# Last Mamba item: key strips issued in three parts, the query side six states sooner, four maxima of attention in the tail

## The reference, cut to what matters

```python
x = x + mamba(layernorm(x))             # 2 layers, 512 channels, 16 states
x = x + cross_attention(layernorm(x), ctx)   # 16 heads of 16
x = x + moe(layernorm(x))               # 8 experts, top 2, and a shared one
# Mamba, per step t, channel e, state n:
v = 0.6 * v + delta * B[n] * xb
h = exp(-delta * exp(a_log)) * h + v
y = sum_n h * C[n]                      # then (y + dp * xb) * silu(z), out projection
# attention: softmax((q k^T) / 4) v, then the output projection
```

## Time and profile before

| | us |
|---|---|
| three timed runs | 1520.03, 1529.7, 1526.61 (median 1526.61) |
| profiled execution | 1523.77 |
| its span in the trace | 1522.3 |
| PE busy | 1374.1 (90%) |
| DVE busy | 1054.2 (69%) |
| ACT busy | 892.6 (59%) |
| POOL busy | 926.5 (61%) |

### The profile page before, as it was taken

One profiled execution on the slowest core, in us unless ns is written; L12 is line 12 of the kernel. 1 busy time (PEld: TensorE's weight loads), 2 busy tenths in 40 slices (PEclk: granted clock), 3 DMA queues, 4 the chain that ended last, 5 costly groups with the idle time before them and its releaser, 6 DMA issues.

```text
span 1522.3 us, 46973 instructions
## 1 busy us (share of the span) xinstructions
PE 1374.1 (90%) x20570; PEld 969.4 (64%) x20570; DVE 1054.2 (69%) x1345; ACT 892.6 (59%) x1303; POOL 926.5 (61%) x809
## 2 busy tenths in 40 slices
PE   5799999999999999999999977789898887999997
PEld 2367776776776776776776765344434344599996
DVE  4698887887887987986986895776676761522224
ACT  3767776776775786776676662145555565434440
POOL 1289989989989989989988968500303000045541
PEclk8799999999999999999999998889999999999999
DMA  5021222212221221122212354540606002512225
GB/s 171 17 75 72 82 86 86 85 59 86 113 82 62 85 86 65 78 86 86 85 59 78 135 136 131 99 95 1 121 5 110 2 1 64 222 53 68 72 63 183
DMA packets 41498, 127.28 MB, mean 84 GB/s; under 512 B 8784, under 2 KB 21584, under 8 KB 32848
## 3 DMA queue, kind: packets, MB, share of 16 engines
q1 hardware_dynamic: 34736, 108.28, 21.8%
q0 software_dynamic: 6048, 14.95, 3.7%
q10 hardware_dynamic: 512, 1.05, 0.4%
HBM read 97.90 MB, written 9.57 MB: 71 GB/s over the span
## 4 chain that ended last, share of the span: by engine, by line
PE 46%; DVE 28%; ACT 11%; issue 9%; DMA 3%; POOL 2%; SPq 2%; DVEq 0%; ACTq 0%
DVE hst L790 13%; PE psum L633 6%; PE psum L1315 4%; PE psum L1727 4%; DVE w_early L790 4%; PE psum L1739 4%; PE psum L610 3%; DVE overlay L681 3%; ACT dA L935 3%; PE psum L572 3%; PE psum L1297 2%; PE psum L507 2%; PE psum L1669 2%; PE psum L1281 2%; DMA overlay<-x_hat,origin 2%
## 5 line engine op out<-in xcount | busy, mean ns | idle before, releaser
L1004 POOL TENSOR_TENSOR hst<-hst,cb 128x512 f32<-128x512 f32 x399 | 510.5, 1304 | 94.6 <-DVE hst L790 79.9
L790 DVE TENSOR_TENSOR_SCAN hst<-dA,psum 128x512 f32<-128x512 f32 x399 | 463.5, 1202 | 108.8 <-PE psum L633 108.7
L610 PE MATMUL psum<-ident,hst 128*128 128x128 f32 x1596 | 236.2, 282 | 15.4 <-POOL hst L1004 12.7
L935 ACT ACTIVATE dA<-delta,alog 128x512 f32<-128x512 f32 x256 | 177.7, 718 | 86.2 <-DVE hst L790 65.4
L935 ACT ACTIVATE dA<-xres,alog 128x512 f32<-128x512 f32 x256 | 176.9, 718 | 70.8 <-DVE hst L790 53.6
L610 PEld LDWEIGHTS psum<-ident,hst 128*128 128x128 f32 x1596 | 174.8, 142 | 63.4 <-POOL hst L1004 21.4
L1436 DVE TENSOR_REDUCE nmax<-psum 128x2 f32<-128x1024 f32 x128 | 154.6, 1221 | 56.9 <-PE psum L1281 56.6
L1365 ACT ACTIVATE pT<-psum 128x1024 f32<-128x1024 f32 x128 | 128.0, 1024 | 103.1 <-PE psum L1301 79.7
L633 PE MATMUL psum<-filt,c_early 64*64 64x86 f32 (+1 forms) x6144 | 145.2, 239 | 20.3 <-DVE hst L790 12.2
L633 PE MATMUL psum<-filt,uT 64*64 64x86 f32 (+1 forms) x6144 | 145.1, 239 | 20.1 <-DVE hst L790 10.8
L633 PEld LDWEIGHTS psum<-filt,c_early 64*64 64x64 f32 x6144 | 124.7, 134 | 57.4 <-issue 40.5
(11 more groups left out here) (234 smaller groups left out, 2102.5 us busy)
## 6 DMA issues: line engine op xcount, KB each, us to landing
cb<-c_rows SPq DMA_DIRECT2D x64, 1024.0 KB, 4.7
qk_first<-w_early SPq DMA_DIRECT2D x64, 64.0 KB, 2.4
qk<-part SPq DMA_DIRECT2D x64, 64.0 KB, 2.7
w_up<-up_dram SPq DMA_DIRECT2D x8, 512.0 KB, 8.0
w_down<-down_dram SPq DMA_DIRECT2D x8, 512.0 KB, 13.7
w_up<-y_choice SPq DMA_DIRECT2D x8, 512.0 KB, 7.0
qk<-part POOLq DMA_DIRECT2D x48, 64.0 KB, 5.1
qk_first<-part SPq DMA_DIRECT2D x40, 64.0 KB, 2.4
```

Of the source, the lines that this page charges most:

```text
L610: m = pe.matmul(psum[:, Y0 + et % EP, t * P:(t + 1) * P], hst(i)[:, t * P:(t + 1) * P], ident[:], start=n == 0 and t == 0, stop=n == NSTAT ...
L790: dve.tensor_tensor_scan(hst(i), a, v, 0.0, ALU.mult, ALU.add).then_inc(scan_done, 1)
L935: act.activation(dA[:, a % NDA, :], delta[k % 2][:, et, :], ACT.Exp, scale=alog[:, k // B, et, n:n + 1]).then_inc(decay_done, 1)
L1004: pool.tensor_tensor(h, h, cb[:, q % 2, state_of(i)[1] % GN, :], ALU.mult).then_inc(g_done, 1)
```

## The change

The key strips are issued as 12, 14 and 6, with the C loads for states 40 to 47 and 48 to 55 between them. The steps of the LayerNorm, `ax` and `aq` move to earlier states. The query strips count on four semaphores instead of one. The first four row maxima of attention (`NMX` = 4, `NMX_RING` = 0) are computed before the border: PE does their matmuls between the quarters of the last output projection, into banks 6 and 7 (one pair for all four, so each waits for the maximum before it), and DVE reduces them behind its last gate product and ahead of the four adds. The opening of attention begins with the fifth.

```diff
-                put(29, "dve", "ln2_aggr")
-                put(33, "act", "ln2_root")
-                put(36, "dve", "ln2_rec")
+                put(28, "dve", "ln2_aggr")
+                put(30, "act", "ln2_root")
+                put(32, "dve", "ln2_rec")
                 for b in range(2):
-                    put(39 + 2 * b, "act", "ln2_scale", b)
+                    put(34 + 2 * b, "act", "ln2_scale", b)
                 for j in range(KD):
-                    put(46 + j, "pe", "ax", j)
-                    put(47 + j, "act", "ax", j)
+                    put(40 + j, "pe", "ax", j)
+                    put(41 + j, "act", "ax", j)
                 for j in range(2):
-                    put(51 + j, "pe", "aq", j)
-                    put(52 + j, "act", "aq", j)
-                    put(52 + j, "dve", "aq", j)
+                    put(46 + j, "pe", "aq", j)
+                    put(47 + j, "act", "aq", j)
+                    put(47 + j, "dve", "aq", j)
...
+            for r in range(NMX):
+                s = 0 if r < NMX_RING else 4
+                steps["dve"].setdefault(("last", s), []).append((NI - 1, "mx", r))
...
                 pe_side(k, "bt", ET - 1)
+                pe_first_max(NMX_RING)
                 bks = [pe_open(k, "bo", t) for t in range(TB)]
...
+                    if NMX_RING + kt + 1 < NMX:
+                        pe_first_max(NMX_RING + kt + 1)
+
+            def pe_first_max(r):
+                j, t = r // TB, r % TB
...
+                else:
+                    pe.wait_ge(y_out, ET * NI)
+                    pe.wait_ge(mx_out, r)
+                if r == 0:
+                    pe.wait_ge(early_k, 16 * 2 * HEADS)
+                if t == 0:
+                    pe.wait_ge(early_q[j], 16 * 2 * HEADS // 4)
+                for e in range(2):
+                    k0 = e * KR
+                    m = pe.matmul(first_pair(r)[:, e, :], qk_first[k0:k0 + KR, 0, j, 0, t * P:(t + 1) * P], qk_first[k0:k0 + KR, 1, j, 0, :],
+                                  start=True, stop=True, tile_position=(k0, 0))
+                m.then_inc(mx_full, 1)
...
+                elif what == "mx":
+                    dve.wait_ge(mx_full, j + 1)
+                    dve.tensor_reduce(nmax[:, 0, j % TB, 2 * (j // TB):2 * (j // TB) + 2], first_pair(j), AX.X, ALU.max, negate=True).then_inc(mx_out, 1)
...
-                        for dst, src in first_strips(1):
+                        for dst, src in strips_k[:12]:
                             sp.dma_start(dst, src).then_inc(early_k, 16)
                     sp_c_load(NUSE * k + 5)
+                    if k == NI - 1:
+                        for dst, src in strips_k[12:26]:
+                            sp.dma_start(dst, src).then_inc(early_k, 16)
                     sp_c_load(NUSE * k + 6)
+                    if k == NI - 1:
+                        for dst, src in strips_k[26:]:
+                            sp.dma_start(dst, src).then_inc(early_k, 16)
                     sp_c_load(NUSE * k + 7)
...
-            for r in range(NSLOT):
-                opening += [(0, "max", r)] + project(1)[r + 2:r + 3 if r < 4 else 0]
+            for r in range(NMX, NSLOT):
+                opening += [(0, "max", r)] + project(1)[r - NMX + 2:r - NMX + 3 if r - NMX < 4 else 0]
```

More of the change, by code:

```diff
@@ L43 @@
 NBLK = 39
+NMX, NMX_RING = 4, 0
 ROUTE_COLS = 592
@@ L67, in banks_for @@
             q, second = second, None
-        elif who == "scan":
+        elif who in ("scan", "mx"):
             q = min((b for b in oldest if b + 1 in oldest), key=lambda b: max(oldest.index(b), oldest.index(b + 1)))
@@ L189, in build @@
         b_qk = sb(ctx, "b_qk", [P, 2, 2])
-        early_k, early_q, early_hi, ld_bqk = sem("early_k"), sem("early_q"), sem("early_hi"), sem("ld_bqk")
+        early_k, early_hi, ld_bqk = sem("early_k"), sem("early_hi"), sem("ld_bqk")
+        early_q = [sem(f"early_q{j}") for j in range(HEADS // 4)]
+        nmax = sb(ctx, "nmax", [P, 2, TB, HEADS // 2])
+        mx_full, mx_out = sem("mx_full"), sem("mx_out")
         KR = 4 * HDIM
@@ L456, in build @@
             plan_back(NI - 1, "last", 0)
+            for r in range(NMX):
+                s = 0 if r < NMX_RING else 4
+                steps["dve"].setdefault(("last", s), []).append((NI - 1, "mx", r))
+            for r in range(NMX_RING):
+                steps["pe"].setdefault(("last", 0), []).append((NI - 1, "mx", r))
             def at_steps(engine, at):
@@ L469, in build @@
                     rows += [(x, TAKER[x[1]]) for x in pair_steps(i) if (x[1] in TILED) == tiled]
-            rows += [(x, TAKER[x[1]]) for x in at_steps("pe", "last")]
+            for k, what, j in at_steps("pe", "last"):
+                rows += [((k, "mx", j), "mx"), ((k, "mx+", j), "mx")] if what == "mx" else [((k, what, j), TAKER[what])]
             place, left_by = banks_for(rows, NRING)
             emptied = {name: n for name, n in zip((x for x, who in rows), ring(rows)[1])}
-            piece_no = {x: n for n, x in enumerate(x for x, who in rows if who != "scan")}
+            piece_no = {x: n for n, x in enumerate(x for x, who in rows if who not in ("scan", "mx"))}
             def bank(*name):
@@ L480, in pe_open @@
                     who, n = left_by[name]
-                    pe.wait_ge({"dve": bank_dve, "act": bank_act, "scan": scan_done}[who], n + n % 2 if who == "scan" else n)
+                    pe.wait_ge({"dve": bank_dve, "act": bank_act, "scan": scan_done, "mx": mx_out}[who],
+                               n + n % 2 if who == "scan" else (n + 1) // 2 if who == "mx" else n)
                 return bank(*name)
@@ L647, in pe_mamba @@
                     pe_add_state(i)
+                    r = i - (NI * TILES - LAG) - 2
+                    if 0 <= r < NMX_RING:
+                        pe_first_max(r)
                     n, et = state_of(i)[1:]
@@ L662, in pe_mamba, with first_pair @@
                             m.then_inc(bank_full, 1)
+                    if NMX_RING + kt + 1 < NMX:
+                        pe_first_max(NMX_RING + kt + 1)
+            def first_pair(r):
+                b0 = place[NI - 1, "mx", r] if r < NMX_RING else Y0
+                return psum[:, b0:b0 + 2, :]
+            def pe_first_max(r):
+                j, t = r // TB, r % TB
+                if r < NMX_RING:
+                    pe_open(NI - 1, "mx", r)
+                    pe_open(NI - 1, "mx+", r)
+                else:
[10 more added lines that the diff above has]
+                m.then_inc(mx_full, 1)
             def tiles_of(k, part):
@@ L1024, in sp_mamba @@
             def sp_mamba():
+                strips_k = list(first_strips(1))
                 sp.dma_start(ident[:], d["ident"]).then_inc(ld_ident, 16)
@@ L1077, in sp_mamba @@
                         sp.wait_ge(bank_dve, emptied_by("dve", k, "aq", 1))
-                        for dst, src in first_strips(0):
-                            sp.dma_start(dst, src).then_inc(early_q, 16)
+                        for n, (dst, src) in enumerate(first_strips(0)):
+                            sp.dma_start(dst, src).then_inc(early_q[n // 8], 16)
                     if k + 1 < NI:
@@ L1084, in sp_mamba @@
                 sp.dma_start(att_w("w_v"), d["w_v"]).then_inc(ld_att, 16)
-                sp.wait_ge(early_q, 16 * 2 * HEADS)
+                for j in range(HEADS // 4):
+                    sp.wait_ge(early_q[j], 16 * 2 * HEADS // 4)
                 sp.dma_start(att_w("w_o"), d["w_o"]).then_inc(ld_att, 16)
@@ L1113, in build @@
             vt = sb(ac, "vt", [P, 2, TB, HEADS * HROW])
-            nmax = sb(ac, "nmax", [P, 2, TB, UH])
             nsplit = sb(ac, "nsplit", [P, TB, P], F32R)
@@ L1270, in pe_max @@
                 o = pair(u, "max", r)
-                if u == 0 and r == 0:
+                if u == 0 and r == NMX:
                     pe.wait_ge(early_k, 16 * 2 * HEADS)
-                    pe.wait_ge(early_q, 16 * 2 * HEADS)
+                    for z in range(HEADS // 4):
+                        pe.wait_ge(early_q[z], 16 * 2 * HEADS // 4)
                 elif r == 0 and half == 0:
```

## The result

| us | before | after |
|---|---|---|
| timed runs, median | 1526.7 | 1516.4 |
| their range | 1520.03 to 1529.7 | 1515.39 to 1516.75 |
| ratio, 95% interval | | 0.9947 [0.9924, 0.9969] |
| span of the profiled execution | 1522.3 | 1514.4 |

By these ratios the change brings 8.1 and 5.5 us (by the medians 10.3 and 6.3); the forecast was 7.7.

The account below looks back on a forecast made before the run. The prediction took the last Mamba item to be bound by POOL's 12.8 us wait on a C load behind 32 key strips. Item -6.0, tail +2.6 and opening -4.3 gave -7.7 from 1525.2: 1517 us, range 1509 to 1524.

Parts of the forecast that it names:

- The stall and its cause: Last Mamba item: POOL waits 12.8 us before state 40 for a C load queued on SP behind 32 key strips.
- The item, 6.0 with the slow clock and 7.4 with the fast: Last Mamba item: gain in POOL's work, 6.0 us with PE at 1.2 GHz, 7.4 at 2.4 GHz.
- the landing of the last key strip: SP's last six strips, behind the second C load: the last lands at 916.3 us, by the median of 2.4.
- rival B: Key strips crawl behind the C loads, landing near 920.5: 1.6 us less gain, 1519 us; chance 0.12.
- the wait that I called covered by 1.5 us: ACT's aq0 waits for the key strips; PE, ready for scan 48 at 920.3, is later by about 1.5 us.
- The tail, +2.6: From POOL's end to the border: four maxima on DVE delay the four adds, 2.6 us longer (bounds 1.7 and 4.6).
- The opening, -4.3: Opening of attention: eight instead of twelve maxima alone save 4.55 us, 4.3 after a small loss.
- 0.2 lost: Opening: PE's second product of maxima after the first score waits for ACT's exponential, held by its strips; 0.2 us.
- the twin with the fast clock: The same forecast with PE at 2.4 GHz in the item: gain there 7.4 us, total given as 1515.5.
- A (nothing takes its place): Rival: no new wait replaces POOL's stall, so all 12.8 us are gained; -14.5 in all, 1511 us; chance 0.18.
- C: Rival: the first C load still lands too late, or POOL waits for it again; -1.7, 1523.5 us; chance 0.09.
- D: Rival: the wait for the key strips becomes the wall for ACT and DVE; +4.0, 1529 us; chance 0.05.

Follow-up runs that it names:

- c_order: The kernel before with only the key strips issued as 12, 14, 6 between the C loads; 1510.78 us, ratio 0.9909.
- strips_first: The changed kernel with all 32 key strips again ahead of the C load; 1525.78 us, ratio 1.0015.
- split_22: The kernel before with only the key strips issued as 12, 10, 10 between the C loads; 1509.0 us, ratio 0.991.
- best_plain: The kernel before with key strips as 12, 10, 10 and 8 instead of 16 of sequence 1's strips on ACT's queue; 1508.63 us, ratio 0.9912.
- few_act: The changed kernel with LayerNorm, ax and aq steps as before, and 8 instead of 16 of sequence 1's strips on ACT's queue; 1509.8 us, ratio 0.9909.
- no_first_max: The changed kernel with all sixteen maxima in the opening and none in the tail; 1514.46 us, ratio 0.9951.
- after_again: The changed kernel unaltered, timed again beside the experiments; 1515.63 us, ratio 0.9964.
- old_plan: The changed kernel with the LayerNorm, ax and aq steps put back to those of before; 1511.77 us, ratio 0.993.
- aq_51: The changed kernel with only the query projection put back to states 51 and 52; 1513.34 us, ratio 0.9933.

## Why the prediction was right, and where its steps were not

*The stall and its cause.* Right, and shown from both sides: c_order takes it away (11.56 us), strips_first brings it back (12.7).

*The item, 6.0 with the slow clock and 7.4 with the fast.* Measured 6.4 at full clock and 5.9 at the slow one: right in kind, the fast case mis-sized by 1. Scan 40 was forecast 16.3 us after S with the slow clock and 14.8 with the fast; it came at 16.06 and 14.32. The bank order held: DVE waits 1.38 or 1.39 before scan 42 in every kernel with the early transposes. The failed term is the landing of the last key strip, put at 26.1 us after S. ACT's aq0 starts at 28.2, released by it. The strip was issued 24.2 us after S, for a forecast of 23.7, but the last six landed after 3.9 to 5.3 us, not 2.4: that is the direction of rival B, though not its size of 30.3. The Trainium skill says, in "DMA: Bandwidth & Descriptors", section "Queues, rings and completion order", that each DMA engine consumes a queue's descriptors in ring order. That strips behind a megabyte land late was drawn from it; the trace agrees, with 4.5 against 2.4 us. So the wait that I called covered by 1.5 us was the last to end in one execution and hidden in the other.

*The tail, +2.6.* Measured +2.7 and +2.3, with the mechanism named: PE feeds a maximum every 2.36 us, and the adds stand behind the fourth. The number is in part luck, since the tail of before ran at a granted clock of 0.83 and those of the changed kernel at 0.94 and 0.96. Where all of it ran at 1.00, it took 10.80 us without maxima (c_order, split_22, best_plain) and 14.24 with four (few_act): +3.4.

*The opening, -4.3.* This step failed as a number. Eight instead of twelve maxima alone took 4.53 us less, as said. But 1.6 of it went at once: behind the border the transposes took 1.72 instead of 1.09, the first product for a maximum 0.79 instead of 0.50 and the first projection 2.64 instead of 1.98, at a fallen clock. The table does not put this down to the maxima: from B the clock fell in five of the eight executions with them and in two of the five without. At like clock B to C is 21.23 against 25.76 at 1.00 and 22.8 against 27.4 at 0.66, so the 4.5 holds. The execution of before had the full clock, both of the changed kernel the fallen one. The "0.2 lost" to ACT's strip queue was too small: PE stood 2.15 us for that bank in one execution and 0.68 in the other. I had compared the queue's end with one bank wait and left out PE's clock in what follows. C to N grows by 1.5 and 3.6 us, and the growth is larger where PE waited less and its clock stayed at 0.50. Net of the opening -1.5 in one execution, +0.6 in the other. How much of this belongs to the queue is open. The five executions with four maxima and 16 strips on ACT have C to N at 38.0 to 42.0, the two with 8 strips at 36.1; but the 36.48 of split_22, with 16 strips and no maxima, shows that the time goes with the clock at least as well as with the count.

*The sum.* -7.7 was forecast; by the pieces it is -5.2 and -3.0, by the two timings -8.1 (0.9947) and -5.5 (0.9964). The forecast of 1517 met 1516.4 by luck: two errors under it, both towards too much gain, and a scatter ahead of S of 2.45 us the other way. In the second group 1515.63 is near it only because before, too, was lower there (1521.93, for the 1525.2 that I counted from). A slip in the sum: the twin with the fast clock comes to 1516.1, not 1515.5. A (nothing takes its place) is refuted for this kernel, but nearly holds for the new queue order alone: 11.56 of 12.8 in the item. C and D did not occur.

## What to carry to other kernels

When an engine waits on a transfer, look first at what stands ahead of it in the issuing queue: splitting 32 small transfers around two large ones was worth 11 us by the medians, and the rest of the edit took five of them back. Work moved earlier to prepare for something meets the waits of its old place sooner; check that the thing prepared for was ever waiting. Work moved across a border out of a busy stretch costs where it goes, even into idle time (here 3.4 us for the 4.5 saved, at like clock), and pays only if what comes next on the other side, here a queue of small transfers on ACT, can start earlier too.

## What the runs showed of the hardware

Small transfers behind a large one in the same queue landed late: the six right behind the second 1 MB load after 3.9 to 5.3 us, the fourteen behind the first after 2.4 to 5.3, and those with only their like ahead after 2.3 to 3.3. ACT needed 21 us to issue 16 such transfers while SP and POOL issued theirs, and 16 us for 8; POOL issued 24 in 11.7.

The small copy that splits the maxima took 0.76 us before, 0.79 in c_order, 0.78 in no_first_max and 0.77 in split_22, and 0.19 or 0.20 in after, after_again and old_plan. In the first four a POOL elementwise operation was running when the copy began, and the copy ended 0.05 to 0.08 us after it (before: POOL until 988.92, copy until 988.97). So it looks like a wait for POOL's operation to end, not a slower copy. In the others POOL was issuing transfers or had not begun it. The rows, before:

```profile
986.54 2.38 POOL L1541 TENSOR_TENSOR xres<-xres,b_o 128x1024 f32<-128x1024 f32 x1
988.21 0.76 DVE L1445 CAST nsplit<-nmax 128x64 fp32r<-128x64 f32 x1
```

and after:

```profile
970.25 11.71 POOL L1567 DMA_DIRECT2D qk<-part  x24 [7.40 <-DVE part L1449]
979.08 0.19 DVE L1495 CAST nsplit<-nmax 128x64 fp32r<-128x64 f32 x1
```

PE's clock fell or not behind a wait of the same length in the same place. In after_again and in aq_51, whose program is the same up to there, PE stood 3.64 and 3.65 us for y0. The sum behind it took 1.09 us in one and 0.63 in the other, and the granted clock of the 8 us from S + 8 was 0.67 and 1.00:

```profile
900.03 1.09 PE L621 MATMUL psum<-ident,hst 128*128 128x128 f32 x4 [3.64 <-ACT xraw L886]
...
901.02 0.63 PE L621 MATMUL psum<-ident,hst 128*128 128x128 f32 x4 [3.65 <-ACT xraw L886]
```

Behind the border it is the same with shorter waits: 1.89 us in c_order (clock 0.66 from B) and in split_22 (1.00), 2.10 in few_act (0.66) and old_plan (1.00). With that, one stretch of unchanged work is 1.6 us longer or shorter from one execution to another (B to C: 25.75 or 27.4 without maxima, 21.23 or 22.8 with four), as much as the effect of the maxima that was in question. Differences under 2 us between two traces of this kernel prove nothing by themselves.
